# Three score banks, one ring of three product banks, another order of jobs, and one reciprocal a pair of heads

## What is computed

```python
# layer 0, per batch
q, k, v = x @ Wq + bq, ctx @ Wk + bk, ctx @ Wv + bv          # 16 heads of 64
ln0 = norm(softmax(q @ k.T / 8, masked) @ v @ Wo + bo + x)
# layer 1
ln1 = norm(ln0 + attention_B(ln0, ln0, mask) @ o_w + o_b)    # 16 heads of 16
ln2 = norm(ln1 + attention_C(ln1, ctx) @ co_w + co_b)        # 16 heads of 16
out = norm(ln2 + relu(ln2 @ lin1_w + lin1_b) @ lin2_w + lin2_b)
```

## Time and profile before

| | |
|---|---|
| median of 3 runs | 1893.57 us (1890.61 to 1894.02) |
| profiled execution | 1884.11 us, span 1882.4 us |
| PE busy | 1739.3 us, 92% of the span |
| DVE, ACT, POOL busy | 69%, 64%, 52% |
| DMA engines of the kernel's queue | 54.1% of 16 engines' span |
| the 12 full bodies | 110.8 us each |

### The profile page before, as it was taken

How to read it: one execution, slowest core, us unless ns; L and a number is a source line. 1 busy time by engine, 2 the same in 40 slices (tenths; PEclk the granted TensorE clock), 3 DMA queues, 4 the chain that set the end, 5 groups by cost and what they waited for, 6 DMA issues and landing times.

```text
span 1882.4 us, 37642 instructions
## 1 busy us (share of the span) xinstructions
PE 1739.3 (92%) x11456; PEld 1298.9 (69%) x11456; DVE 1304.5 (69%) x5194; ACT 1197.7 (64%) x3985; POOL 986.1 (52%) x1030
## 2 busy tenths in 40 slices
PE   7799999999999999999999999999999999998887
PEld 5666677676766767677676776767677676776565
DVE  4365777686867768676777768778676877757863
ACT  3264676666666676766666676666766666666752
POOL 3143555646555464655546464555646555454842
PEclk9999999999999999999999999999999999999989
DMA  7421416575665857566575756757576675703110
GB/s 156 116 91 64 141 64 218 159 248 167 207 214 165 264 168 237 168 201 227 164 259 162 222 174 197 243 161 260 147 229 196 189 244 164 225 29 124 68 57 12
DMA packets 223174, 319.97 MB, mean 170 GB/s; under 512 B 31488, under 2 KB 192000, under 8 KB 214784
## 3 DMA queue, kind: packets, MB, share of 16 engines
q1 hardware_dynamic: 219856, 317.55, 54.1%
q10 hardware_dynamic: 3120, 0.01, 0.1%
HBM read 166.49 MB, written 151.00 MB: 169 GB/s over the span
## 4 chain that ended last, share of the span: by engine, by line
PE 53%; DVE 17%; DMA 13%; SPq 6%; ACT 5%; issue 5%; POOL 0%; DVEq 0%; POOLq 0%; ACTq 0%
PE ps_gd L657 22%; PE ps_ga L657 9%; PE ps_s L777 7%; PE ps_t L794 7%; PE ps_av L817 7%; DMA p_kept<-blocks 6%; DVE prob L1076 5%; DMA prob_b<-p_kept 4%; ACT prob L899 3%; SPq L570 3%; SPq L553 3%; DVE blocks L1099 2%; DMA k_parts_B<-k_hl 2%; DVE res_ln L1052 2%; DVE stats_ln L1037 2%
## 5 line engine op out<-in xcount | busy, mean ns | idle before, releaser
L1201 POOL TENSOR_TENSOR prob<-prob,recip 128x512 f32<-128x512 f32 x768 | 786.3, 1045 | 729.4 <-DVE recip L1087 725.0
L899 ACT ACTIVATE prob<-prob,ext 128x256 f32<-128x256 f32 x1536 | 757.7, 499 | 45.0 <-DVE ext L1076 42.8
L909 ACT ACTIVATE prob_t<-ps_t 128x512 f32<-128x512 f32 x384 | 227.0, 595 | 388.4 <-PE ps_t L794 387.2
L794 PE MATMUL ps_t<-ident,prob 128*128 128x128 f32 x1920 | 305.7, 284 | 5.3 <-DVE prob_b L1108 5.1
L899 ACT ACTIVATION_READ_ACCUMULATOR prob<-prob,ext 128x1 f32 x1536 | 295.0, 192 | 0.0
L794 PEld LDWEIGHTS ps_t<-ident,prob 128*128 128x128 f32 x1920 | 219.4, 142 | 89.7 <-issue 44.0
L1076 DVE CUSTOM_DVE_ANT_0 prob<-ps_s,mask_a 128x256 f32<-128x256 f32 x512 | 186.7, 421 | 117.0 <-PE ps_s L777 113.3
L1076 DVE CUSTOM_DVE_ANT_0 prob<-ps_s,mask_b 128x256 f32<-128x256 f32 x512 | 186.7, 420 | 85.3 <-PE ps_s L777 84.4
L1076 DVE CUSTOM_DVE_ANT_0 prob<-ps_s,zero 128x256 f32<-128x256 f32 x512 | 185.9, 419 | 69.7 <-PE ps_s L777 69.7
L1099 DVE STREAM_TRANSPOSE blocks<-prob 128x512 f32<-128x512 f32 x288 | 185.3, 681 | 7.7 <-DMA p_kept<-blocks 7.3
L777 PE MATMUL ps_s<-k_ctx,q 64*128 64x256 f32 x1024 | 145.5, 402 | 12.2 <-DVE ext L1076 7.6
(11 more groups left out here) (98 smaller groups left out, 2779.4 us busy)
## 6 DMA issues: line engine op xcount, KB each, us to landing
p_kept<-blocks SPq DMA_DIRECT2D x576, 128.0 KB, 2.4
prob_b<-p_kept SPq DMA_DIRECT2D x144, 512.0 KB, 3.4
k_parts_C<-k_hl SPq DMA_DIRECT2D x64, 256.0 KB, 4.5
k_parts_B<-k_hl SPq DMA_DIRECT2D x64, 256.0 KB, 2.8
k_B<-k_parts_B SPq DMA_DIRECT2D x16, 1024.0 KB, 6.3
q_parts_B<-q_hl SPq DMA_DIRECT2D x64, 256.0 KB, 6.4
q_B<-q_parts_B SPq DMA_DIRECT2D x16, 1024.0 KB, 5.4
q_parts_C<-k_hl SPq DMA_DIRECT2D x64, 256.0 KB, 6.6
```

The lines of the kernel that those rows point to most:

```text
L794: last = nc.tensor.transpose(two(ps_t[e])[:, kt, qt * P:(qt + 1) * P], src[:, e, qt, kt * P:(kt + 1) * P], ident[:, :])
L899: last = nc.scalar.activation(tile, tile, ACT.Exp, bias=ext[:, slot, e, t:t + 1], scale=-1.0, accum_out=sums[:, slot, e, t:t + 1])
L909: nc.scalar.activation(prob_t[:, e], two(ps_t[e]), ACT.Copy).then_inc(copied_second, 1)
L1201: nc.gpsimd.tensor_tensor(rows, rows, recip[:, slot, e].unsqueeze(2) .to_broadcast([P, TT, TOK]), ALU.mult).then_inc(normed[s], 1)
```

## The change

Seven things change; the last body keeps its order, the arithmetic is the same.

1. **Three score banks.** In full bodies the two heads of a pair take two of three banks in turn (`score_bank`), the third is the former `ps_av`. A score waits for the first head of the pair before it instead of for both.
2. **Weighing shares a bank.** In full bodies `W` writes into `ps_t[1]`, the bank of `T1`. `T1` gets a new wait: for the `AV` of the last `W`.
3. **One ring of three product banks** for all jobs, instead of a ring of two for DVE's and one bank for ACT's.
4. **The table of jobs** is rearranged.
5. **One reciprocal a pair** (128x4), after both heads' exponentials; POOL waits for it once.
6. `load` gets one more wait (`taken["xT"]`).
7. **Start:** job `k 1` moves behind the first score, and in the second body `load` and `res0` come first.

```diff
-        ("A", 0): late + [job("ks"), dma("save k", "B"), ln("ln1")],
-        ("A", 1): [dma("k", "B"), job("qs"), dma("save q", "B")],
-        ("A", 2): [dma("q", "B"), job("x2T"), job("v", 0)],
-        ("A", 3): [job("qc"), dma("save q", "C"), job("k", 2), job("q", 2)],
+        ("A", 0): late + [dma("save k", "B"), job("ks"), dma("save q", "B")],
+        ("A", 1): [dma("k", "B"), job("qs"), ln("ln1"), job("v", 0)],
+        ("A", 2): [job("x2T"), dma("q", "B"), job("q", 2), job("qc"), io("value_c")],
+        ("A", 3): [job("k", 2), dma("save q", "C"), job("v", 1)],
         ("A", 4): [dma("q", "C"), job("oc"), job("vs")],
-        ("A", 5): [io("value_c"), ln("ln2"), job("v", 1)],
+        ("A", 5): [ln("ln2")],
         ("B", 0): [job("x3T"), job("v", 2)],
-        ("B", 1): [job("hd"), job("h", 0), res("res3", 0)],
-        ("C", 0): [job("h", 1), res("res3", 1)],
-        ("C", 1): [job("q", 3), res("res2", 0)],
-        ("B", 2): [job("h", 2), res("res2", 1)],
-        ("B", 3): [job("k", 3), res("res1", 0)],
-        ("A", 6): [half("y"), res("res1", 1)],
-        ("A", 7): [job("y"), res("res0", 0)],
-        ("C", 2): [io("load"), job("v", 3), ln("ln3")],
-        ("C", 3): [io("store"), job("kc")],
-        ("B", 4): [job("vc")],
-        ("B", 5): [io("save_c"), job("xT")],
-        ("B", 6): [job("cT")] + [half("wo")] * closed,
+        ("B", 1): [res("res3", 0), res("res3", 1), job("h", 0)],
+        ("C", 0): [job("hd")],
+        ("C", 1): [job("h", 1), job("q", 3), res("res2", 0), res("res2", 1)],
+        ("B", 2): [],
+        ("B", 3): [res("res1", 0), job("k", 3), job("h", 2)],
+        ("A", 6): [half("y"), res("res1", 1), res("res0", 0)],
+        ("A", 7): [],
+        ("C", 2): [job("y")],
+        ("C", 3): [io("load"), job("kc")],
+        ("B", 4): [job("v", 3), io("save_c"), io("store"), job("vc")],
+        ("B", 5): [job("xT"), job("cT"), ln("ln3")],
+        ("B", 6): [half("wo")] * closed,
         ("B", 7): [job("wo")] * closed,
-        ("C", 4): [ln("ln0"), job("q", 0, "x")] * closed,
-        ("C", 5): [job("k", 0, "x")] * closed,
-        ("C", 6): [job("q", 1, "x")] * closed,
+        ("C", 4): [job("k", 0, "x")] * closed,
+        ("C", 5): [job("q", 0, "x")] * closed,
+        ("C", 6): [job("q", 1, "x"), ln("ln0")] * closed,
         ("C", 7): [job("k", 1, "x")] * closed,
     }
 
+    if present == {"x", "a"}:
+        after = {place: [x for x in jobs if x[1:3] not in (("res0", 0), ("load", 0))] for place, jobs in after.items()}
+        after["A", 0] = [job("k", 1)] + after["A", 0]
+        head += [res("res0", 0), io("load")]
+    if present == {"x"}:
+        first = first[:3]
...
+        def score_bank(body, step, e):
+            if body.full:
+                return (ps_s + [ps_av])[(2 * body.place(step) + e) % 3]
+            return ps_s[e]
+
+        def weigh_bank(body):
+            return ps_t[1] if body.full else ps_av
...
-                    pe.wait_ge(masked[s0], count(b0, HEADS, 2 * p0 + 2))
+                    same = body.full and (body.pairs.index(step) or body.before.full)
+                    pe.wait_ge(masked[s0], count(b0, HEADS, 2 * p0 + (1 if same else 2)))
...
+                if e == 1:
+                    last = [x for x in body.steps[:body.steps.index(step)] if x[0] == "W"]
+                    if last and body.full:
+                        pe.wait_ge(ctx_out[last[-1][1]], count(body.batch(last[-1]), QUADS, last[-1][2] + 1))
...
             def wait_bank_free(body, step):
-                past = body.earlier(step, 2 if step[1] in DVE_JOBS else 1, ring[step[1]])
+                past = body.earlier(step, 3, lambda s: s[0] == "J" and s[1] != "mask")
...
-                for e in range(2):
-                    dve.wait_ge(exped[s], count(body.batch(step), HEADS, 2 * p + e + 1))
-                    nc.vector.reciprocal(recip[:, slot, e], sums[:, slot, e]).then_inc(recipd[s], 1)
+                dve.wait_ge(exped[s], count(body.batch(step), HEADS, 2 * p + 2))
+                nc.vector.reciprocal(recip[:, slot], sums[:, slot]).then_inc(recipd[s], 1)
...
+                pool.wait_ge(recipd[s], count(body.batch(step), PAIRS, p + 1))
                 for e in range(2):
-                    pool.wait_ge(recipd[s], count(body.batch(step), HEADS, 2 * p + e + 1))
```

More of the change, by code:

```diff
@@ L274, in __init__ @@
         self.pairs = [s for s in self.steps if s[0] == "S"]
-        self.banks = [s for s in self.steps if s[0] == "J" and s[1] in DVE_JOBS]
+        self.banks = [s for s in self.steps if s[0] == "J" and s[1] != "mask"]
         self.by_blocks = (before.by_blocks if before else []) + [
@@ L320, in earlier @@
             return None
-        if self.present == set("xabcm"):
+        if self.full:
             assert past[i] == mine[i]
@@ L457, in jobs_of @@
             return DVE_JOBS.get(name) or ACT_JOBS[name]
-        ring = {**{n: (lambda s: s[0] == "J" and s[1] in DVE_JOBS) for n in DVE_JOBS},
-                **{n: (lambda s: s[0] == "J" and s[1] in ACT_JOBS) for n in ACT_JOBS}}
         def bank_of(body, step):
-            if step[1] in ACT_JOBS:
-                return ps_ga
-            return ps_gd[(body.base[1] + body.banks.index(("J",) + step[1:])) % 2]
+            return ps_g[(body.base[1] + body.banks.index(("J",) + step[1:])) % 3]
         LN_AFTER = {"wo": "ln0", "os": "ln1", "oc": "ln2", "y": "ln3"}
@@ L772, in scores @@
                     (_, s0, p0, _), b0 = past
-                    pe.wait_ge(masked[s0], count(b0, HEADS, 2 * p0 + 2))
+                    same = body.full and (body.pairs.index(step) or body.before.full)
+                    pe.wait_ge(masked[s0], count(b0, HEADS, 2 * p0 + (1 if same else 2)))
+                if body.full and not body.before.full and step == body.pairs[0]:
+                    _, s0, quad0, _ = weighing = [x for x in body.before.steps if x[0] == "W"][-1]
+                    pe.wait_ge(ctx_out[s0], count(body.before.batch(weighing), QUADS, quad0 + 1))
                 for t in range(TT):
@@ L776, in scores @@
                         r = slice(HALF * e, HALF * (e + 1))
-                        last = nc.tensor.matmul(two(ps_s[e])[:, t, :], q[r, t * P:(t + 1) * P], k[r],
+                        last = nc.tensor.matmul(two(score_bank(body, step, e))[:, t, :], q[r, t * P:(t + 1) * P], k[r],
                                                 start=True, stop=True)
@@ L791, in turn @@
                     pe.wait_ge(copied_second, 2 * (quad - 1) + e + 1)
+                if e == 1:
+                    last = [x for x in body.steps[:body.steps.index(step)] if x[0] == "W"]
+                    if last and body.full:
+                        pe.wait_ge(ctx_out[last[-1][1]], count(body.batch(last[-1]), QUADS, last[-1][2] + 1))
+                    elif not last and body.before and body.before.full:
+                        last = [x for x in body.before.steps if x[0] == "W"]
+                        pe.wait_ge(ctx_out[last[-1][1]], count(body.before.batch(last[-1]), QUADS, last[-1][2] + 1))
                 for kt in range(TT):
@@ L824, in weigh @@
                     pe.wait_ge(v_loaded, count(b, 16, 16))
+                ps = weigh_bank(body)
                 past = body.earlier(step, 1, lambda x: x[0] == "W")
@@ L833, in weigh @@
                                 h = 4 * (quad % 2) + 2 * j + e
-                                last = weighted(two(ps_av)[e * DH0:(e + 1) * DH0, j, :],
+                                last = weighted(two(ps)[e * DH0:(e + 1) * DH0, j, :],
                                                 v0[:, kt, h * DH0:(h + 1) * DH0], j, e, kt)
@@ L866, in job @@
                 b = body.batch(step)
-                ps = two(ps_ga)
+                ps = two(bank_of(body, step))
                 act.wait_ge(filled[name], count(b, jobs_of(name), i + 1))
@@ L919, in evac_weighed @@
                         c = 2 * quad + j
-                        last = nc.scalar.activation(k0_ctx[:, c, :], two(ps_av)[:, j, :], ACT.Identity,
+                        last = nc.scalar.activation(k0_ctx[:, c, :], two(weigh_bank(body))[:, j, :], ACT.Identity,
                                                     bias=col["bv0"][:, c:c + 1])
@@ L1076, in extremes @@
                         last = nc.vector.tensor_tensor_reduce(
-                            out=prob[:, slot, e, t, :], in0=two(ps_s[e])[:, t, :], in1=mask,
+                            out=prob[:, slot, e, t, :], in0=two(score_bank(body, step, e))[:, t, :], in1=mask,
                             scale=-SCALE[s], scalar=BIG, op0=ALU.add, op1=ALU.min,
```

13 lines of the change are left out of this document (7 added, 6 removed).

## The result

The changed kernel takes **1824.87 us** (median, 1821.01 to 1834.03); the kernel before, beside it on the same chip, 1893.80 us. The ratio is 0.9644 with an interval of 0.9604 to 0.9683. The forecast of 1878.5 us had the sign right and under a quarter of the size; its range ended at 1846.

What follows compares the result with a forecast made beforehand. PE was taken as the bound, with 73 us idle of 1300 us. The terms -37.7 + 4.2 + 21.0 - 2.5 = -15.0 us took the span from 1882.4 to 1867.4, scaled to 1878.5 us; range 1846 to 1906.

Steps and rivals of the forecast that it cites:

- The score waits: PE's waits on DVE ahead of B4, C7 and A6 go, by the third bank and moved `ln3`, `ln0`: -37.7 us.
- `wo` stays: The first half of `wo` still waits for ACT's copy of the last weighing of A: 0 us.
- `T1`: `T1` waits for the weighing's `AV` at B2, and B3's score waits for DVE: 0.35 us a body, +4.2 us.
- The DMA stretch: From `save k` to the load for B1's weighing, PE arrives 1.73 us earlier at a late load: +21.0 us.
- I let the two cancel: the load lands where it did: At B1, `value_c`'s 0.9 us offsets what earlier `save q` can win back; PE waits 1.75 us longer a body.
- rival (a): `save q` right behind `save k` closes the gaps between DMAs, and PE waits as before: 1851 us, chance 0.25.
- The ring of banks: A job's product bank was filled a place ago, so the three-bank ring gives 0 us; at most 8 us.
- the waits on product banks of before are none of PE's three: In the profile before, PE's three listed waits include none on a product bank, so the term is 0 us.
- One reciprocal: On DVE one 128x4 takes 154 ns; POOL's wait for the second head is hidden: 0 us.
- Start: `k 1` fills the wait behind the first score, and the second body's `load` goes out sooner: -2.5 us.
- the scaling: The profiled execution, forecast at 1869.1 us, was scaled by the 0.5% between profile and median before, to 1878.5 us.

Runs made afterwards that it cites:

- the banks alone: The changed kernel with the table of jobs, the start and the two reciprocals of the kernel before, so only the banks are new: 1862.49 us, ratio 0.9875.
- the table alone: The kernel before with the new table of jobs, the new start and the new wait of `load`, old banks and two reciprocals: 1864.90 us, ratio 0.9885.

## Why the prediction was right or wrong

Its sum beside what the two profiles show. The eleven bodies from the first to the twelfth `wo` of the full bodies take 1219.3 us before and 1173.9 after; "measured" is the difference of PE's listed waits in them, by releaser. Half clock: the granted clock gives 13.4 us at 1.2 GHz before and 10.1 after, of which half counts.

| term | forecast | measured |
|---|---|---|
| scores waiting for DVE, and the 0.21 us of A6 | -37.7 (12 bodies) | -35.5 (11 bodies) |
| `wo` waiting for ACT | 0 | +0.5 |
| `T1` behind the weighing, B2 and B3 | +4.2 | none listed |
| waits on `prob_b` | +21.0 | -6.7 |
| `x3T` waiting for `ln2` | not seen | +3.3 |
| batch loads | 0 | +0.9 |
| half clock | 0 | -1.7 |
| not in any listed wait | 0 | -6.2 |
| start, up to the first `wo` | -2.5 | -1.9 |
| end | 0 | -2.8 |
| **sum** | **-15.0** | **-50.1** |

**The score waits: right**, in place and size. Both mechanisms work as put: 0.7 us a wait by the third bank (35.1 to 19.3 with the banks alone), the rest by the new table, with `ln3` and `ln0` moved (18.1 with the table alone; 15.5 us come back when only the third bank is given up).

**`wo` stays: right.** 1.11 us after, in the same place. (In the twelfth body it is hidden: PE waits there 0.9 us for a batch load just ahead.) That the chain from `T1` over the exponentials sets it was argued there; the kernel that puts work between `T1` and `wo` takes the whole wait away, and shows it.

**`T1`: too dear.** At B2, `T0` and `T1` stand back to back, with no idle time listed; PE's timeline of after, and ACT's copy that it had to wait for:

```profile
758.79 1.30 PE L820 MATMUL ps_t<-ident,prob 128*128 128x128 f32 x8
```

```profile
758.48 0.84 ACT L947 ACTIVATE k_ctx<-ps_t,col_bv 128x256 f32<-128x256 f32 x2 [0.73 <-PE ps_t L843]
```

The copy ends at 759.32; `T0` and `T1` together take 1.30 us, and elsewhere 0.60 to 0.66 each. So at most 0.1 us is in it, and the bound of 0 was the value.

**The DMA stretch: the step that failed** is "I let the two cancel: the load lands where it did", and with it the term of +21.0 us, which measured -6.7. Three of its four numbers held. In the bodies shown PE arrives 1.4 us sooner (forecast 1.73); A3's weighing lets `value_c` go 23.1 us after the start of A0 (23.0); the load for A5 goes out at 23.6 as before. With the old order of DMAs even the total held, 43.4 us. Missing was what `save q` ahead of `k_B` does to the loads. I wrote that it "helps `q_B`", and then looked for the gain in the 13% of idle engine time, as if bytes were the limit; against rival (a) I held that `save q` of C is issued no sooner. That is true (+24.0 in both), but it **lands** sooner, as less of `q_B` is in front of it, and B1's load goes out 1.7 us sooner on the mean of the eleven bodies. That is about what PE gains, so the wait at B1 stays (1.4 us a body before, 1.3 after) instead of growing by 1.75. At A5 the load goes out as before, but `q_B` is 4.4 us further ahead of it, and 5.8 us of waits become 0.6. Together -6.7. After's 14.9 us hang on few bodies: one wait of 4.3 us is in them, and the kernel with two reciprocals has 10.7. The stretch was bound by a chain of waits in one queue, not by what the engines move. The rule of the ring order that I brought up against `value_c` holds for `save q` in the other direction, and there it has the larger lever: a whole read of 1 MB instead of 0.25 MB.

Rival (a), PE waits as before, was the case, at 0.25 of the chances. It named the right edit, "`save q` right behind `save k` closes the gaps". On the spans its sum is -15.0 - 21 - 6.7 = -42.7 us against the measured -50.1; most of the way from its 1851 us to the 1824.87 is the scaling, below.

**The ring of banks: 0 us was wrong as its worth**, though right as a wait: no product waits for a bank in after. The step "the waits on product banks of before are none of PE's three" shows that the old order has no use for the ring. It doesn't say what the new order would cost without it: 24 us, 12 of them in the listed wait. The forecast of the change as a whole didn't suffer, since both came together.

**One reciprocal: right as far as the runs tell**, 0 us forecast and no wait listed. 174 ns for 128x4 lies nearer to the 154 of one 128x2 than to two of them; I took 154. The Trainium skill ("VectorE: DVE Perf Modes", the section on the TRN2 errata) has a fixed cost an instruction, whatever its size; the rows agree in the main and show 20 ns for two more elements a partition.

**Start: right in the sum**, -1.9 of -2.5. Its parts moved more: PE waits 12.06 us for the second batch behind the MLP weights, against 5.7 in before, and makes it good before the first `wo`.

**Three things were left out.** The wait of `x3T` (+3.3) belongs to the table: it is there with the table alone too (4.2 us, 12 times). `ln2` kept its place, but job `v 1`, which lay between it and `x3T` on PE, moved to A3; that this is the cause is argued, not shown. The -6.2 us not in any listed wait, 0.6 a body, I can't place. Idle time that the modelled ends of the matmuls cover would look so, but no run here shows it. And the scaling: I carried before's 0.5% between profile and median over to after, whose profile is 0.5% above its own. Of the 53.6 us between 1878.5 and 1824.87, 35 are the sum's error and the other 18 that.

## What to carry to other kernels

Where a stretch of DMAs looks full (87% busy here), follow one queue and ask of each DMA what it waits for and what is in front of that: a write that a large read-back waits for belongs ahead of the previous large read, and here the gain was handed on along the chain. One body is not the mean: the body shown had gained 2.6 us, the eleven 1.7. Restoring the issue order alone is the cheap test of it. Judge banks together with the order they allow: a wait that the old order's trace doesn't have says nothing of what a bank is worth in the new one.

## What the hardware showed that I had not expected

- Four writes of 256 KB, issued one place sooner, move the kernel by 2.4%: 6.4 us from issue to landing behind a 1 MB read, 3.5 ahead of it.
- A DMA engine share of 0.87 was no limit: in the bodies shown the same stretch moves 298 GB/s instead of 282 with the new order, and PE waits less.
- A long wait can cost more than itself. Behind the 4.30 us wait at 535 us the granted clock is 0.70 over the next 8 us (the window shown above), so part of them ran at 1.2 GHz: its weighing takes 1.97 us instead of 1.08. The row of PE's timeline of after:

```profile
535.14 1.97 PE L843 MATMUL ps_t<-prob_b,v 128*64 128x256 f32 x8 [4.30 <-DMA prob_b<-p_kept]
```
